# Second attention: the fills for the scores go to the end of TensorE's steps

## The reference

```python
q = (x @ wq_w.T + wq_b).reshape(B, T, H, Dh)      # B = 2, T = 1024, H = 16, Dh = 8
k = (x @ wk_w.T + wk_b).reshape(B, T, H, Dh)
v = (x @ wv_w.T + wv_b).reshape(B, T, H, Dh)
scores = jnp.einsum('bthd,bshd->bhts', q, k) * scale
key_mask = (x[:, :, 0] != PAD_ID)[:, None, None, :]
scores = jnp.where(key_mask, scores, -jnp.inf)
attn = jax.nn.softmax(scores, axis=-1)
out = jnp.einsum('bhts,bshd->bthd', attn, v).reshape(B, T, C)
return out @ wo_w.T + wo_b
```

## Time and profile before

| | |
|---|---|
| median of 3 runs | 1957.23 us (1950.94 to 1958.64) |
| profiled execution | 1955.24 us, span 1953.4 us |
| PE, DVE, ACT, POOL busy over the span | 1628.1, 1444.0, 1262.6, 974.4 us |
| second attention, turn -1 (maxima only) | to about 1502.8 us |
| its turns 0 to 6 | 1502.8 to 1847.1 us |
| its block 7 (scores only) | 1847.1 to 1885.9 us |
| rest (last output product, channel mixer) | to 1953.4 us |

### The profile page before, as it was taken

One profiled execution on the slowest core, in us unless ns is written; L12 is line 12 of the kernel. 1 busy time (PEld: TensorE's weight loads), 2 busy tenths in 40 slices (PEclk: granted clock), 3 DMA queues, 4 the chain that ended last, 5 costly groups with the idle time before them and its releaser, 6 DMA issues.

```text
span 1953.4 us, 27210 instructions
## 1 busy us (share of the span) xinstructions
PE 1628.1 (83%) x9867; PEld 661.5 (34%) x9867; DVE 1444.0 (74%) x2199; ACT 1262.6 (65%) x2078; POOL 974.4 (50%) x637
## 2 busy tenths in 40 slices
PE   2899999999999999999999999833576777777763
PEld 1334444444434443444443444322441111111112
DVE  2678777777777877777777777596679777777608
ACT  1677777777777777777777777611052777777751
POOL 1577777777777777777777777720000011111110
PEclk8899999999999999999999999965685999999986
DMA  3111111111111111111111111000010000000000
GB/s 95 31 28 33 33 33 33 33 28 33 33 33 32 31 30 38 29 30 35 28 33 38 28 33 29 17 2 0 1 38 1 7 13 13 12 13 13 13 18 22
DMA packets 68107, 50.82 MB, mean 26 GB/s; under 512 B 27187, under 2 KB 56918, under 8 KB 67974
## 3 DMA queue, kind: packets, MB, share of 16 engines
q1 hardware_dynamic: 67974, 49.07, 11.1%
HBM read 28.79 MB, written 1.31 MB: 15 GB/s over the span
## 4 chain that ended last, share of the span: by engine, by line
PE 62%; issue 14%; DVE 13%; ACT 6%; POOL 2%; SPq 2%; DMA 0%; POOLq 0%; ACTq 0%; DVEq 0%
PE PS L1209 15%; PE PS L1221 14%; PE PS L1232 13%; DVE mxp L1110 4%; PE PS L1251 4%; PE PS L1241 3%; PE PS L1259 3%; ACT ering L649 3%; ACT va L660 2%; PE PS L1245 2%; DVE on L850 2%; PE PS L1477 2%; PE PS L1422 2%; DVE st L797 1%; POOL on L574 1%
## 5 line engine op out<-in xcount | busy, mean ns | idle before, releaser
L825 DVE TENSOR_REDUCE nmx<-PS 128x1 f32<-128x1024 f32 x512 | 625.4, 1222 | 212.1 <-PE PS L1210 206.1
L513 POOL TENSOR_TENSOR ering<-ering 128x1024 f32<-128x1024 f32 x256 | 603.7, 2358 | 21.4
L649 ACT ACTIVATE ering<-PS,nmx 128x1024 f32<-128x1024 f32 x512 | 572.6, 1118 | 2.9 <-DVE nmx L825 2.1
L511 POOL TENSOR_SCALAR ering<-ering,rho 128x1024 f32<-128x1024 f32 x256 | 286.6, 1119 | 300.9 <-DVE rho L834 300.9
L1209 PE MATMUL PS<-region 64*128 64x512 f16 x1536 | 420.4, 381 | 1.0 <-ACT ering L649 1.0
L1210 PE MATMUL PS<-region 64*128 64x512 f16 x1536 | 420.4, 381 | 0.0
L1110 DVE TENSOR_REDUCE mxp<-PS 128x2 f32<-128x1024 f32 x256 | 302.8, 1222 | 79.1 <-PE PS L1463 79.0
L1221 PE MATMUL PS<-ident,ering 128*128 128x128 f32 x2048 | 330.6, 284 | 11.4 <-ACT t L660 2.5
L759 ACT ACTIVATE ering<-PS 128x1024 f32<-128x1024 f32 x256 | 259.3, 1025 | 108.8 <-PE PS L1446 107.9
L1221 PEld LDWEIGHTS PS<-ident,ering 128*128 128x128 f32 x2048 | 222.0, 140 | 303.1 <-POOL ering L513 99.1
L660 ACT ACTIVATE t<-PS 128x512 f32<-128x512 f32 x256 | 152.6, 596 | 88.7 <-PE PS L1221 88.7
(11 more groups left out here) (251 smaller groups left out, 1708.7 us busy)
## 6 DMA issues: line engine op xcount, KB each, us to landing
region<-region SPq DMA_DIRECT2D x128, 128.0 KB, 2.3
osb<-scr SPq DMA_DIRECT2D x32, 256.0 KB, 4.1
rcp<-scr SPq DMA_DIRECT2D x32, 256.0 KB, 4.1
rcp<-scr SPq DMA_DIRECT2D x64, 64.0 KB, 2.0
x<-in_L_attn_X SPq DMA_DIRECT2D x4, 256.0 KB, 3.7
wq_raw<-in_L_attn_Wq SPq DMA_DIRECT2D x16, 64.0 KB, 2.5
wk_s<-in_L_attn_Wk SPq DMA_DIRECT2D x16, 64.0 KB, 1.8
wo_s<-in_L_attn_Wo SPq DMA_DIRECT2D x32, 32.0 KB, 3.2
```

The costliest lines, as they stand in the source:

```text
L511: P.tensor_scalar(e2, e2, rho[:, s:s + 1], 1.0, ALU.mult, ALU.mult).then_inc(s_scl_ok, 1)
L513: P.tensor_tensor(e1, e1, e2, ALU.subtract).then_inc(s_sub_ok, 1)
L649: A.activation((E1, E2)[p][s % 4], PS[:, bank:bank + 2, :].rearrange("p a b -> p (a b)"), ACT.Exp, bias=nmx[:, 2 * s + p:2 * s + p + 1], s ...
L825: V.tensor_reduce(nmx[:, 2 * s + p:2 * s + p + 1], PS[:, bank:bank + 2, :].rearrange("p a b -> p (a b)"), AX.X, ALU.max, negate=True).then ...
```

## The change

In each step TensorE's call of `scores1(n, t)` goes from directly behind `maxima1` to the end of the step, behind PV, the spread and OUT where the step has them. Nothing else is changed, and the other engines' lists stay.

```diff
--- before.py
+++ after.py
@@ -1493,8 +1493,6 @@
                 for t in range(32):
                     if nxt:
                         maxima1(n + 1, t)
-                    if own:
-                        scores1(n, t)
                     if t == 1 and n >= 1:
                         values1(n - 1, 15)
                     if t % 2 == 1 and t > 1 and own:
@@ -1515,6 +1513,8 @@
                         if nxt:
                             pe.wait_ge(s_ct_ev1, 2 * (n + 1) + 1)
                         to_out1(2 * n)
+                    if own:
+                        scores1(n, t)
 
 
             pe.wait_ge(s_y1_ok, 4 * G1)
```

## The result

The changed kernel takes 1966.7 us (median of 20 runs), the kernel before 1957.6. The ratio of the times is 1.0042, 95% interval 1.0032 to 1.0051: slower by 0.4%, some 9 us. One of the 20 runs of the kernel before, at 2719.1 us, is in the slow state, which the ratio leaves out. The profiled execution has a span of 1964.8 us, 11.4 more than before. The forecast was 1954, some 3 us under the kernel before.

A forecast was written before the change was run, and what follows sets the result against it. No engine is full in blocks 0 to 6, so a ring of waits sets the pace. From 1955.24 us, minus 10.1 there, plus 7.7 in block 7, gives 1952.8; run median 2 higher, 1954.8, stated as 1954, range 1943 to 1968.

The forecast's parts named there:

- Part (a): Plain pair of steps in blocks 0 to 6: 2.81 us instead of 3.03, a gain of 0.22 per pair.
- the ring: Waits setting the new plain pair: odd scores fill, its exp, next odd maxima fill, PV, odd scores fill; 2.81 us.
- Part (b): Steps 3 and 19: scores wait with PV for the osb copy, 4.12 us from Sc(1) to Sc(3), +1.31.
- (c): Steps 14 and 30: output product OUT stands before the scores fill; its pair takes 3.12 us, +0.31 over plain.
- (d): Half block of 16 steps: 24.10 us against 24.74, gain 0.64; blocks 0 to 6 together gain 10.1 us.
- Part (e): Block 7, without maxima: a new ring of 2.49 us a pair, 45.9 us against 38.2, loss 7.7.
- rival 3: TensorE's clock falls in block 7: 1.05 us more on 16 pairs, 17 us, time 1971; chance 0.10.
- Part (f): Everything behind the last osb copy stays as it was, 68 us.
- 1 (stall absorbed): The stall at the osb copy is absorbed: 17 us less, 1937; chance 0.14.
- 2 (new ring no shorter): Blocks 0 to 6: the new ring of waits is no shorter than the old, time 1977.5; chance 0.10.
- 4 (no effect): The moved fill changes nothing: VectorE waits for Max as before and block 7 catches up, 1957; chance 0.06.
- the wide one: The whole time's range of 1943 to 1968 us, taking in the milder half of the first two rivals.

The follow-up runs named there:

- 7: As 1, but the fill for scores is issued twice in odd steps, an extra fill on the supposed ring; 1972.6 us, ratio 1.0074.
- 8: As 1, but the fill for scores is issued twice in even steps; 1952.5 us, ratio 0.9970.
- Kernel 4: As 1, and in steps 3 and 19 too the scores stand directly behind the maxima; 1936.3 us, ratio 0.9875.
- kernel 3: The changed kernel plus three extra unsignalled score fills ahead of the waiting PV in each odd step of block 7; 1960.2 us, ratio 1.0000.
- 1: The changed kernel with the old order (scores directly behind the maxima) back in block 7 only; 1951.0 us, ratio 0.9957.
- 2: The kernel before with the new order in block 7 alone, old order in blocks 0 to 6; 1972.5 us, ratio 1.0073.
- 5: As 1, with ScalarE's osb copy of steps 2 and 18 moved in front of that step's exp; 1935.1 us, ratio 0.9878.
- 6: As 1, with both the early osb copy and, in steps 3 and 19, scores directly behind the maxima; 1925.8 us, ratio 0.9830.

## Why the prediction was right or wrong

**Part (a), the plain pair: right.** 2.83 us against 2.81, the wait is the one named, and 7 and 8 show the ring. The 0.02 lies between the exp and the next Max, 1.08 from start to start where 1.02 + 0.04 were put down.

**Part (b), the osb copy: right.** A stall of +1.31 was forecast, 4.12 us from Sc(1) to Sc(3); it is 4.13, or +1.30 over a plain pair. Kernel 4 takes 1.08 of it away where 1.0 to 1.3 were expected. What the part left out is that a gap of this kind, some 1 us behind 0.7 of waiting, can cost the clock too: two of the 14 half blocks were longer by about 1 us.

**Parts (c) and (d): right but for the dips.** The pair with OUT is 3.13 us against 3.12. A half block is 24.22 us against 24.10, mostly the 0.02 of each pair; its gain is 0.52 instead of 0.64. Over 13 that is 1.6 us, and the two dips make 2.1. Together they are 3.7, about the 10.1 - 6.7 = 3.4 that are missing.

**Part (e), block 7: wrong in size, and this made the result.** The ring was right (8.0 us by kernel 3, 7.7 forecast; 2.51 a pair at full clock against 2.49). The term was priced with a clock at 1.00 throughout, and measured 15.6 instead of 7.7. The step that failed is the one that priced every pair of block 7 at 2.49 us: five of them took 3.59. With it the sum's sign went wrong, a gain of some 3 us forecast and a loss of 9 measured. The clock was set aside as rival 3, at 0.10, for the reason that it is 1.00 today though TensorE is idle 8 of 39 us there. That reason was bad: the new schedule doesn't keep those gaps, it adds one of 0.9 us in each pair and makes the one at osb 2.35 us, where it was 1.73. Rival 3 was the true mechanism, and its mark (granted clock of block 7 under 0.8) is met by 0.78. Its price for a pair was right (1.05; 1.08 measured), its number of pairs was not: the clock rose again at OUT and stayed up for most of the second half, so 7.7 us (by kernel 3) were paid instead of 17.

The Trainium skill, in TensorE: Matmul & The Clock Gate (A second HAM failure mode), has a kernel that cycles through PSUM banks, with short idles between groups of matmuls, going to and fro between the clock levels. This trace agrees: 0.50 from 1849 to 1867, 1.00 at 1870 to 1874, 0.71 at 1874 to 1878.

**Part (f)** held within 0.8 us.

**The rivals and the range.** 1 (stall absorbed) fell by kernel 4: it costs 1.08 a half block. 2 (new ring no shorter) fell by the pair of 2.83 us. 4 (no effect) fell by the same pair and by block 7's 53.8 us. The time of 1966.7 is outside the forecast's own range of 1949 to 1960. That it lies inside the wide one, at its upper end, is luck: rival 3 at its full price of 1971 would not. The sum with the measured sizes is 1957.6 - 6.7 + 15.6 = 1966.5. Changes under some 10 us were said to be out of reach of a measurement; with 20 runs of each kernel the interval of 1.0032 to 1.0051 leaves no doubt that the change makes it slower.

Three readings in the working are off by a little, and nothing hangs on them: the merged row of 2.36 us holds two reductions 1.13 us apart (2.36 - 1.23), not 1.18; PV to its follower at full clock, 1729.89 to 1730.78, is 0.89; and the PV at 1858.06 comes 0.03 behind the exp that ended at 1858.03.

## What to carry to other kernels

When an order is changed for the sake of one stage, look at every stage that runs the same loop: here the order that wins in blocks 0 to 6 loses in the block where one of the two streams is missing, and a condition on the block turns the change from 0.4% slower into 0.4% faster. Anything moved behind an instruction that waits inherits its wait, so list the rare waits (here the osb copy) as well as the plain ones; two lines for them gave a further 1.3%. And when TensorE gets new gaps, price the stage at both clock levels with the rows of the slow level, rather than as an unlikely case.

## What the runs showed of the hardware

All this is the granted clock of the ten traces between the first osb copy and the last. It falls to 0.50 13 times there, each time 0.5 to 1.7 us behind the start of an osb copy, where TensorE waits for it. In blocks 0 to 6 TensorE's gap in front of that PV is 1.01 or 1.06 us in the changed kernel and in 1, 3, 7 and 8: 7 falls at 65 copies. In the kernel before and in 2, 4, 5 and 6 no gap at these copies is over 0.90 us: no fall at 65. In block 7 it fell at both gaps of 2.35 us, at one of two of 2.31 and at three of four of 1.98, and not at the eight from 1.66 to 1.78, nor at the four of 0.86 and 1.06 in kernels 5 and 6. So the length of the gap alone doesn't decide, and what else does was not tried.

The gaps of 0.90 us in the plain pairs of block 7 did not bring it down there: with them it stayed at 1.00 from 1880 to the end of the block in the changed kernel, and from 1878 on in kernel 2, there over a second osb gap of 2.31. Once down in the first half of block 7, it stayed at 0.50 in the changed kernel from 1849 to 1867 with TensorE busy 14.55 of 18.00 us, and in kernel 2 from 1858 to 1875 with 13.54 of 17.00; at this level the gaps of these pairs are 0.69 us. Both times it came back during OUT, which followed a fill without a gap. The second return in the changed kernel, by 1879.47, came without one, so OUT is not what a return needs.

Filling the gaps with work of no use made the kernel faster (1966.7 to 1960.2 us). One of the changed kernel's 20 runs took 1951.5 us, at a mean granted clock of 0.938 where the others have 0.93; it left no trace, so it isn't known where its clock stayed up.
